# A six-stage two-layer model: the eight-expert layers' second weights loaded during stage three, their first weights stored in two parts, ten instead of thirteen split chunks in stage one, and the bias products in other places of TensorE's order

## The reference

```python
x = x + 0.5 * _L0_ffn_ref(_layernorm(x), gate_w, w_gate, w_up, w_down)     # 2 experts, top 1
x = x + _L0_attn_ref(_layernorm(x), Wq, bq, Wk, bk, Wv, bv, Wo, bo)        # 16 heads, causal
x = x + 0.5 * _L0_ffn_ref(_layernorm(x), gate_w, w_gate, w_up, w_down)
x = x + 0.5 * _L1_ffn_ref(_layernorm(x), rw1, rw2, w1, b1, w2, b2)         # 8 experts, top 2
x = x + _L1_attn_ref(_layernorm(x), in_proj_w, conv_w, ...)                # state-space mixer
x = x + 0.5 * _L1_ffn_ref(_layernorm(x), rw1, rw2, w1, b1, w2, b2)
```

```python
logits = _gelu(x @ rw1) @ rw2
wgt, idx = jax.lax.top_k(softmax(logits), 2)
for e in range(8):
    Ye = _gelu(x @ w1[e] + b1[e]) @ w2[e] + b2[e]
    Ce = _gelu(b1[e]) @ w2[e] + b2[e]
    for k in range(2):
        mask = idx[..., k] == e
        active = jnp.any(mask).astype(x.dtype)
        out = out + active * wgt[..., k:k + 1] * jnp.where(mask[..., None], Ye, Ce)
```

## Time and profile before

| | before |
|---|---|
| median of 3 runs | 1039.83 us (1039.57 to 1041.65) |
| the profiled execution | 1041.49 us |
| its span | 1039.5 us |
| mean granted TensorE clock in the span | 0.934 of full speed (2.4 GHz) |
| busy: PE, PEld, DVE, ACT, POOL | 857.8, 556.2, 596.7, 396.5, 492.4 us |
| HBM read, written | 106.11 MB, 35.16 MB |

### The profile page before, as it was taken

The page is one execution under the profiler, slowest core; times in us unless marked ns, Lnnn a source line. Parts: engine busy times, 40 slices in busy tenths (PEclk is TensorE's granted clock), DMA queues, the critical chain, the costliest instruction groups (busy, mean ns, idle before and its releaser), DMA issues.

```text
span 1039.5 us, 21523 instructions
## 1 busy us (share of the span) xinstructions
PE 857.8 (83%) x7798; PEld 556.2 (54%) x7799; DVE 596.7 (57%) x1105; ACT 396.5 (38%) x955; POOL 492.4 (47%) x538
## 2 busy tenths in 40 slices
PE   3099976787778679998589999969689978999995
PEld 2046642332323335664389999633434444799994
DVE  5623336688796242334535655648389845655655
ACT  6322223145557242224234444356401125344441
POOL 2228868048888331213235454223588733455531
PEclk9999988998978889998879999999899988999997
DMA  8313443235656810002946665330000001766644
GB/s 293 108 42 113 124 128 121 108 94 184 187 174 213 320 59 14 31 21 88 412 163 244 240 221 203 97 137 1 0 0 1 1 1 45 275 221 244 244 167 137
DMA packets 47752, 142.25 MB, mean 137 GB/s; under 512 B 10577, under 2 KB 23714, under 8 KB 41154
## 3 DMA queue, kind: packets, MB, share of 16 engines
q0 software_dynamic: 19280, 93.40, 26.7%
q1 hardware_dynamic: 22366, 40.92, 11.0%
...
HBM read 106.11 MB, written 35.16 MB: 136 GB/s over the span
## 4 chain that ended last, share of the span: by engine, by line
PE 51%; POOL 13%; DMA 12%; DVE 11%; issue 7%; ACT 5%; SPq 1%; POOLq 0%; ACTq 0%; DVEq 0%
PE psum L563 15%; PE psum L536 12%; PE psum L522 8%; PE psum L1826 4%; POOL mem L1538 4%; POOL mem L1536 3%; DMA mem<-w2l_dram 2%; DMA stage<-in_w 2%; POOL mem L246 2%; PE psum L509 1%; PE psum L1853 1%; PE psum L114 1%; DVE mem L1449 1%; DVE mem L315 1%; DVE psum L2033 1%
## 5 line engine op out<-in xcount | busy, mean ns | idle before, releaser
L563 PE MATMUL psum<-mem 128*128 x1536 | 178.9, 273 | 3.7 <-DVE mem L801 2.5
L563 PEld LDWEIGHTS psum<-mem 128*128 128x128 f16 x1536 | 146.3, 98 | 23.9 <-issue 4.7
L912 POOL DMA_INDIRECT y_dram<-mem x64 | 63.4, 991 | 150.4 <-DVE mem L817 147.6
L536 PE MATMUL psum<-mem 128*128 128x128 f16 x2208 | 132.4, 220 | 0.0
L536 PEld LDWEIGHTS psum<-mem 128*128 128x128 f16 x2208 | 128.6, 99 | 0.7
L653 ACT ACTIVATE mem<-psum,mem 128x128 f32<-128x128 f32 x368 | 105.1, 369 | 55.1 <-PE psum L536 53.6
L907 POOL DMA_INDIRECT mem<-xn_dram,mem x64 | 65.8, 1029 | 113.8 <-PE psum L509 85.9
L1403 ACT ACTIVATE mem<-psum 128x512 f32<-128x512 f32 (+1 forms) x160 | 79.9, 552 | 77.0 <-PE psum L1299 50.8
L522 PE MATMUL psum<-mem 128*128 x432 | 102.7, 397 | 0.7 <-issue 0.7
L1449 DVE TENSOR_REDUCE mem<-psum 128x2 f32<-128x1024 f32 (+2 forms) x96 | 87.6, 949 | 20.4 <-PE psum L1273 12.2
L114 PE MATMUL psum<-ones 128*128 128x512 f16 x326 | 92.3, 413 | 0.6 <-issue 0.6
...
## 6 DMA issues: line engine op xcount, KB each, us to landing
...
```

What stands on the lines that cost most here:

```text
L536: ins = eng.matmul(c.bank(2 * p + j // half)[:, j % half * P:(j % half + 1) * P], mats[q][:, l, k, j * P:(j + 1) * P], x[:, p, k, :], star ...
L563: ins = eng.matmul(c.bank(6)[:, 0:D], a[:, 0 if gated else p, q * half + j, :], w[:, at], start=(i == 0), stop=(i == 3 * CF - 1))
L912: eng.indirect_dma_start(c.y_dram[:, :], bass.IndirectOffsetOnAxis(ap=yidx[:, b:b + 1], axis=0), yo[:, b % 2, :], None).then_inc(s_ys[b % ...
```

## The change

- `W1_FIRST` is 10 instead of 13: three chunks move on GpSimd from stage one's blocks to the beginning of stage two.
- `store_w1(eng, i)` now stores one quarter (two experts, two DMAs of 1 MB). Quarters 0 and 1 stand on the SP queue in stage one, ahead of the load of its rows, and wait for chunks 5 and 9. Quarters 2 and 3 stand in stage two behind the last projection store and ahead of the first `max_rows`, and wait for chunks 13 and 17. The rows of b1 are stored by `store_b1` at the beginning of stage two's SP code.
- Stage three takes its work area from `mem1` instead of `mem2`, and VectorE waits for all of w1's stores before it. The load of w2 (`load_w2`) stands on SP ahead of stage three's own code and waits for `begun`, the end of the first products of its first block.
- The bias products are cut into 16 parts of 16 matmuls. Ten stand on TensorE ahead of stage four's layer norm, each with one `keep_awake` matmul behind it, in place of the 28 that stood there (`lead`); six stand in place of ten `keep_awake` matmuls ahead of the tables' last product. They go to bank 2. The Gelu of b1 (ScalarE) and its two halves (now VectorE, before GpSimd) stand ahead of the layer norm, their sum on VectorE is further forward. `idle` is 16 in both eight-expert stages, before 0 in stage four; these matmuls go to bank 0.
- One copy of b2 (`load_cb`) is loaded behind stage three, and waited for at the end of stage four.

```diff
-        if "idle_before" in src:
+        if lead and "idle_before" in src:
...
+        if W["bias_part"] is not None:
+            keep_awake(c, eng, 3, 4)
+            for i in range(10):
+                W["bias_part"](eng, i)
+                keep_awake(c, eng, 3, 1)
...
-        if not W["first_time"]:
+        if W["bias_part"] is not None:
+            keep_awake(c, eng, 3, 8)
+        elif not W["first_time"]:
...
-        if not W["first_time"]:
+        if W["bias_part"] is not None:
+            for i in range(10, 16):
+                W["bias_part"](eng, i)
+                keep_awake(c, eng, 3, 1)
+        elif not W["first_time"]:
...
-        if not gated:
...
-            W["bias_pe"](eng)
...
-            keep_awake(c, eng, 2, W["idle"])
+            keep_awake(c, eng, 0, W["idle"])
...
+            W["bias_wait"](eng)
...
+        if not gated:
+            W["bias_dve"](eng)
...
-    s_rows = n("rows", 16 * 5)
-    def store_w1(eng):
-        eng.wait_ge(*w1_split["done"](w1_split["count"]))
-        rows = A["w1_rows"].rearrange("(e p) c -> p e c", p=P)
-        for i, w in enumerate((w1_h, w1_l)):
-            w = w.bitcast(F32).rearrange("p (e c) -> p e c", e=E1)
-            for a in (0, E1 // 2):
-                part = slice(a, a + E1 // 2)
-                eng.dma_start(rows[:, part, i * KD * FF // 2:(i + 1) * KD * FF // 2], w[:, part, :]).then_inc(s_rows.sem, 16)
-        eng.dma_start(A["w1_rows"][:, KD * FF:KD * FF + CF], A["b1slab"]).then_inc(s_rows.sem, 16)
+    def load_w2(eng):
+        eng.wait_ge(*s_rows(16 * 9))
+        eng.wait_ge(*mem2_free)
-        eng.dma_start(cb[E1:2 * E1, :], A["b2"]).then_inc(s_in.sem, 16)
+        eng.wait_ge(*begun)
...
+    def load_cb(eng):
+        eng.wait_ge(*x_done)
+        eng.dma_start(cb[E1:2 * E1, :], A["b2"]).then_inc(s_cbin.sem, 16)
...
-        eng.wait_ge(*s_in(64))
+        eng.wait_ge(*s_in(48))
...
-    def bias_pool(eng):
+    def bias_halves(eng):
...
-    def bias_pe(eng):
...
-        eng.wait_ge(*s_gz(2))
-        eng.wait_ge(*s_w2(64))
-        for a in range(KD):
-            for e in range(E1):
-                i = 0
-                for j in range(CF):
-                    at = e * CF * D + j * D + a * P
-                    for w in (w2_h, w2_l):
-                        col = 2 * (a * E1 + e)
-                        ins = eng.matmul(c.bank(6)[:, col:col + 2], w[:, at:at + P], gz[:, e, j, :], start=(i == 0), stop=(i == 2 * CF - 1))
-                        i += 1
-        ins.then_inc(s_c.sem, 1)
+    BIAS = [(a, e, j, w) for a in range(KD) for e in range(E1) for j in range(CF) for w in (w2_h, w2_l)]
...
+    def bias_part(eng, i):
...
+        if i == 0:
+            eng.wait_ge(*s_gz(2))
+            eng.wait_ge(*s_w2(64))
+        n = len(BIAS) // 16
+        for a, e, j, w in BIAS[n * i:n * (i + 1)]:
+            at, col = e * CF * D + j * D + a * P, 2 * (a * E1 + e)
+            ins = eng.matmul(c.bank(2)[:, col:col + 2], w[:, at:at + P], gz[:, e, j, :], start=(j == 0 and w is w2_h),
+                             stop=(j == CF - 1 and w is w2_l))
+        if i == 15:
+            ins.then_inc(s_c.sem, 1)
...
+    def bias_wait(eng):
...
-        sums = c.bank(6)[:, 0:2 * KD * E1].rearrange("p (a e l) -> p a e l", a=KD, l=2)
+        sums = c.bank(2)[:, 0:2 * KD * E1].rearrange("p (a e l) -> p a e l", a=KD, l=2)
...
-    stage_ = dict(sync=sync, store_w1=store_w1)
+    stage_ = dict(sync=load_cb, act=bias_act, dve=bias_halves, load_w2=load_w2)
...
+        store_w1(eng, 2)
+        store_w1(eng, 3)
...
-W1_FIRST = 13
+W1_FIRST = 10
...
+        s_rows = c.sem("w1_rows_stored", 16 * 9)
...
+        def store_b1(eng):
+            eng.dma_start(A["w1_rows"][:, KD * FF:KD * FF + CF], A["b1slab"]).then_inc(s_rows.sem, 16)
...
+        def store_w1(eng, i):
...
+            eng.wait_ge(*split1["done"](1 + 4 * (i + 1)))
+            rows = A["w1_rows"].rearrange("(e p) c -> p e c", p=P)
+            part = slice(2 * i, 2 * i + 2)
+            for j, w in enumerate((w1_h, w1_l)):
+                w = w.bitcast(F32).rearrange("p (e c) -> p e c", e=E1)
+                eng.dma_start(rows[:, part, j * KD * FF // 2:(j + 1) * KD * FF // 2], w[:, part, :]).then_inc(s_rows.sem, 16)
...
-                st = moe_stage(c, st, E0, TOP1, NB0, True, W0, Region(mem2, mats_at), w1_during if n == 0 else None,
+                if n > 0:
+                    progs.append(dict(dve=lambda eng: eng.wait_ge(*s_rows(16 * 9))))
+                st = moe_stage(c, st, E0, TOP1, NB0, True, W0, Region(mem2, mats_at) if n == 0 else Region(mem1, mats_at), w1_during if n == 0 else None,
...
-                               split0["sync"] if n == 0 else None)
+                               (lambda eng: (split0["sync"](eng), store_w1(eng, 0), store_w1(eng, 1))) if n == 0 else None)
...
-                    mixer_at = keep.at
-                    weights, W1 = l1_weights(c, A, stage, split1, w2_stored, w1_h, w1_l, w2_h, w2_l, rr_h, rr_l, rw2, cb, keep,
-                                             [st["done"](st["count"]), split1["done"](split1["count"])], slabs)
-                    progs.insert(w1_at, dict(sync=weights["store_w1"]))
+                    mixer_at = l1_at = keep.at
+                    tail = Region(mem1, 4 * E1 * KD * FF)
+                    tail.at = mats_at
+                    weights, W1 = l1_weights(c, A, stage, split1, w2_stored, w1_h, w1_l, w2_h, w2_l, rr_h, rr_l, rw2, cb, tail,
+                                             mem2_free, st["begun"], st["done"](st["count"]), s_rows, slabs)
+                    progs.insert(w1_at, dict(sync=weights["load_w2"]))
...
-                    l1_at = keep.at
...
-                W1 = dict(W1, bias_pe=lambda e: None, bias_act=lambda e: None, bias_dve=lambda e: None, bias_pool=lambda e: None,
-                          bias_turn=lambda e: None, bias_add=lambda e: None, idle=16)
+                W1 = dict(W1, bias_part=None, bias_wait=lambda e: None, bias_dve=lambda e: None, bias_turn=lambda e: None, bias_add=lambda e: None)
...
+                progs.append(dict(sync=store_b1))
...
-                                     w1_rest)
+                                     w1_rest, store_w1)
...
+                mem2_free = st["done"](st["count"])
```

29 lines of the change are left out of this document (12 added, 17 removed).

## The result

| | kernel before | changed kernel |
|---|---|---|
| median of 4 runs each, one chip | 1040.45 us | 1028.64 us |
| range | 1039.57 to 1041.65 | 1023.95 to 1029.65 |
| span of the profiled run | 1039.5 us | 1027.6 us |

The ratio is 0.9872, with a 95% interval of 0.9852 to 0.9892: 11.8 us faster, where 13.5 were forecast, and inside the range. On a second chip the changed kernel had 0.9891 (0.9838 to 0.9944).

What follows compares the result with a forecast made beforehand. TensorE had half of the chain; the largest stall touched was the wait for w2 in stage four's opening. Terms -13.0 - 3.0 + 5.0 - 2.5 = -13.5 us, off the median of 1039.83, gave 1026.3 us, range 1019 to 1031.5.

Steps and rivals of the forecast that it cites:

- Stage four's opening: Early w2 gives stage four's opening the last stage's order, bias products hidden: -13.0 us, between -13.6 and -7.2.
- Load of w2 beside stage three: The 8.4 MB load beside stage three's nine blocks stays hidden: 0, a few us if gathers came later.
- End of stage one: Three fewer GpSimd chunks let the last scatter go earlier, until TensorE limits: -3.0 us, bounds -3.0 and +2.
- Start of the heads: In stage two, 4.19 MB of w1 stores ahead of the first write of maxima delay the first scores: +5.0 us.
- Rival 2: Start of stage two's heads: the maxima's write waits for its engines' whole share, 7.1 us; 1028.4 us, chance 0.18.
- End of stage two: Without w1 stores w2's pieces land earlier and TensorE sets the rows' update: -2.5 us, up to -4.
- Rival 3: Stage four's opening: TensorE's clock replaces w2 as limit, 5.8 us less gain; 1032.1 us, or part, from 1029; chance 0.13.

Runs made afterwards that it cites:

- kernel before, split: The kernel before the change, with the first three stacks' loads in parts of 16 rows and stack zero's issues shared by SP and ScalarE; ratio 0.9996.
- early quarters: The changed kernel with the stores of w1 quarters 2 and 3 moved ahead of SP's wait for the last projection stores; ratio 0.9909.
- split stacks: The changed kernel with each load of the first three stacks (3 x 16 rows) issued as three loads of 16 rows; ratio 0.9831.
- second trace: The changed kernel itself, unaltered, run and traced once more on a chip where the kernel before took 1050 us; ratio 0.9891.

## Why the prediction was right, step by step

**Stage four's opening**, -13.0: the size was right (-12.6 between the two marks, -12.9 for the whole stage), and the way there partly. The bias parts ended at 482.2 where 482.1 was worked out, hidden as told, but that agreement is luck: stage three's last product ended at 473.9 and not at 474.7, and from there the parts and their wide matmuls took 8.3 us and not 7.4, as the clock fell at 478.3. The 16 wide matmuls took 5.8 us, not 3.4 to 4.0; only some 2 us of it lay on the path, since the rows landed at about 17 us behind L712 anyway. The prediction named the wait for w2 first and took the products' own time as hidden behind it. With the early load alone the gain was 4.4 us (up to 5.6 with VectorE's order as before); the other 7 to 8.1 us of the 12.6 came with the moved products.

**Load of w2 beside stage three**, 0: from the update to the y loads of stage three are 118.0 to 119.7 us in the kernels with that load beside it, 119.2 and 118.3 in the two without. The term was nothing, as forecast.

**End of stage one**, -3.0: it was -2.2. The last scatter is 3.55 us behind the start of TensorE's last second product, as read from stage three, but that product began at 137.59, not 136.82. The two quarters' stores lie among the chunk loads: with 13 chunks one load took 7.1 and 7.2 us and the y loads came 1.3 and 0.4 us later than before. The y loads of the kernel before, split, came at 144.77, 1.1 us earlier than in the kernel before with the same stage one, so one pair of traces gives this term only to about 1 us.

**Start of the heads**, +5.0: it was +7.2 between the marks (+6.7 against the layer norm). This step failed in size and in its clock. The stores began at 202.5, not at 196 in this trace's time: I had taken 8.4 us to landing, the median in rows 10, for the last projection stores, which took 14.1, behind the stacks' loads. Rows 9 held the better number: SP's next instruction, which waits for that landing, came 14.3 us behind the last of them (191.0 to 205.26). The stores then had the DMAs to themselves, 4.19 MB in 10.5 us, and the write of maxima landed when they were through. So it was the wait and not the stacks' share that made the delay in this order; the early quarters show that the share gives the same end in the other. The mechanism behind both is the three engines. The Trainium skill's rule (DMA: Bandwidth & Descriptors, "Why a DMA increments its semaphore by 16 and not by 1") that a copy is spread over the largest number of engines up to 16 that divides the slowest dimension of both its sides is borne out by the changed kernel, the early quarters and the split stacks: 74 to 84 GB/s of 400 and a busy share of 0.19 to 0.21 for loads of 3 x 16 rows, 12.7 us of landing for a small write behind them, and once all three stacks' loads have 16 rows no such stretch, and 4.6 to 6.7 us for that write among the stores. Rival 2, which that rule gives, was nearer (7.1) than my middle value. The 5.0 had no mechanism of its own: it lay between one at 0 and one at 7.1, and the runs showed the second.

**End of stage two**, -2.5: it was -4.1 from the first scores to the update, -5.5 in the second trace, and down to -9 in others. The wait for w2 is gone as told. The rest is TensorE's own heads, about 1.5 us shorter in the first trace. They are not shorter by fewer waits: TensorE was busy for 112.1 us of them and not 114.3, and idle for 24.5 and not 23.8, at a mean clock of 0.91 instead of 0.89. Whether the w1 stores, now gone from the heads' end, have to do with the clock was not tried; the kernel before, split, which still has them, was busy for 112.0 us at 0.90.

**What had no term.** The coefficient products cost 1.0 and 1.3 us more. The same kernel gave 4.98 and 5.02 us in one trace, 5.12 and 3.72 in the other, and all kernels between 3.72 and 5.97: this goes with the granted clock over these instructions (0.72 and 0.73 after, 0.98 and 0.92 before, 0.61 where they took 5.97), not with the change, since one kernel gave both. Rival 3 had the right place for a low clock and the wrong price. Between the sum and the spans (-11.9) lie 1.6 us: the heads' start +1.6, stage one +0.8, the end of stage two -1.6, stage three -1.1, and behind stage four +1.8.
